# Basis table of a quarter period, layer 0 as a dense product before its mixing, and fp32r parts in place of fp32

## Time and profile before

| what | value |
|---|---|
| median of 3 runs | 227.8 us |
| the profiled execution's own time | 227.68 us |
| its span, first to last instruction | 225.5 us |
| PE busy | 220.1 us (98%) |
| DVE, ACT, POOL busy | 98.8, 75.0, 110.1 us |
| moved by DMA | 20.42 MB, 91 GB/s in the mean |

### The profile page before, as it was taken

One profiled execution on the slowest core, in us unless ns is written; L12 is line 12 of the kernel. 1 busy time (PEld: TensorE's weight loads), 2 busy tenths in 40 slices (PEclk: granted clock), 3 DMA queues, 4 the chain that ended last, 5 costly groups with the idle time before them and its releaser, 6 DMA issues.

```text
span 225.5 us, 3597 instructions
## 1 busy us (share of the span) xinstructions
PE 220.1 (98%) x1212; PEld 185.2 (82%) x1212; DVE 98.8 (44%) x147; ACT 75.0 (33%) x199; POOL 110.1 (49%) x133
## 2 busy tenths in 40 slices
PE   7799999999999999999999999999999999999995
PEld 2568888888888888888888888888888888888884
DVE  4246444344544343445443444454434444544334
ACT  2067233333322333333223333332233333322211
POOL 4757754355566545445665454456654544522200
PEclk9999999999999999999999999999999999999999
DMA  6931022333222323322233323221232332212112
GB/s 201 310 99 52 9 96 96 102 93 84 72 53 96 99 96 99 99 63 88 52 96 99 96 99 99 71 81 52 96 99 96 99 99 81 73 49 90 47 49 93
DMA packets 13543, 20.42 MB, mean 91 GB/s; under 512 B 2618, under 2 KB 4538, under 8 KB 13538
## 3 DMA queue, kind: packets, MB, share of 16 engines
q1 hardware_dynamic: 10642, 18.16, 25.3%
q0 software_dynamic: 2048, 1.05, 2.4%
q10 hardware_dynamic: 848, 1.14, 1.5%
HBM read 11.96 MB, written 8.39 MB: 90 GB/s over the span
## 4 chain that ended last, share of the span: by engine, by line
PE 95%; DMA 3%; DVE 0%; ACTq 0%; issue 0%
PE f_ps L443 26%; PE y_ps L423 26%; PE f_ps L453 13%; PE f_ps L460 13%; PE f_ps L465 13%; DMA basis_sb<-in_fourier_basis 3%; PE a_ps L481 2%; PE a_ps L408 1%; PE y_ps L417 0%; DVE x L392 0%; PE a_ps L460 0%; PE f_ps L417 0%; PE a_ps L465 0%; ACTq L260 0%; ACTq L259 0%
## 5 line engine op out<-in xcount | busy, mean ns | idle before, releaser
L224 POOL TENSOR_TENSOR x<-x_in,bias 128x512 f32<-128x512 f32 x32 | 40.9, 1278 | 81.0 <-issue 46.9
L217 POOL DMA_INDIRECT gathered<-in_L_cond_weights,row_now x58 | 56.5, 974 | 13.2 <-issue 10.1
L443 PE MATMUL f_ps<-a_high,y_high 128*128 128x512 f32 x128 | 53.8, 420 | 0.0
L443 PE MATMUL f_ps<-a_low,y_high 128*128 128x512 f32 x128 | 50.3, 393 | 0.0
L358 DVE TENSOR_TENSOR x<-f_ps,x 128x512 f32<-128x512 f32 x32 | 22.1, 692 | 49.4 <-PE f_ps L443 47.9
L286 ACT ACTIVATE y_high<-y_ps 128x512 fp32r<-128x512 f32 x32 | 19.1, 597 | 69.6 <-PE y_ps L423 69.6
L282 ACT ACTIVATE y_high<-y_ps 128x512 fp32r<-128x512 f32 x32 | 19.1, 597 | 61.4 <-PE y_ps L423 61.4
L460 PE MATMUL f_ps<-b_sign,y_high 128*128 128x512 f32 x124 | 36.5, 415 | 0.0
L423 PEld LDWEIGHTS y_ps<-blocks,x_in 128*128 128x128 f32 x256 | 33.5, 191 | 3.5 <-issue 0.7
L423 PEld LDWEIGHTS y_ps<-blocks,x 128*128 128x128 f32 x256 | 33.4, 191 | 3.2 <-DVE x L358 0.5
L453 PE MATMUL f_ps<-a_high,y_low 128*128 128x512 f32 x128 | 35.1, 396 | 0.0
(11 more groups left out here) (44 smaller groups left out, 73.0 us busy)
## 6 DMA issues: line engine op xcount, KB each, us to landing
x_in<-in_x SPq DMA_DIRECT2D x31, 256.0 KB, 2.7
out_x<-x SPq DMA_DIRECT2D x31, 256.0 KB, 2.0
gathered<-in_L_cond_weights,row_now POOLq DMA_INDIRECT x58, 2.4
w_sb<-in_L_ffn_W_base SPq DMA_DIRECT2D x1, 512.0 KB, 7.5
w_sb<-in_L_ffn_W_base ACTq DMA_DIRECT2D x1, 512.0 KB, 8.9
basis_sb<-in_fourier_basis SPq DMA_DIRECT2D x1, 257.0 KB, 3.3
basis_sb<-in_fourier_basis ACTq DMA_DIRECT2D x1, 257.0 KB, 6.7
bias<-in_L_ffn_b_base SPq DMA_DIRECT2D x1, 256.0 KB
```

The source lines that it names most:

```text
L217: nc.gpsimd.indirect_dma_start(gathered[:, slot, layer, :], None, mix_rows[layer], IndirectOffsetOnAxis(rows[:, layer:layer + 1].bitcast(u ...
L224: nc.gpsimd.tensor_tensor(out=x1[:, slot, :], in0=x_in[:, slot, :], in1=bias[:, :], op=ALU.add).then_inc(biased, 1)
L443: last = nc.tensor.matmul(f0_ps[:, :], y0_high[:, k * P:(k + 1) * P], a[:, k, :], start=(k == 0 and a is a_high), stop=(k == CHUNKS - 1 an ...
```

## The change

- The basis table has a quarter period (129 columns) for all 512 coefficients, half the bytes of before, in one DMA. The product with it is eight matmuls into four banks; DVE builds the four quarters of the spectrum from sums and differences.
- `enc` is loaded twice, to rows 0 and 64 of one tile, and turned into one fp32r tile: high part above, low part below. The spectrum, too, is split. enc x spectrum is then two fp32r products for each of the four banks.
- `masks` goes first in ACT's queue, `kinds` second, then the two `enc` loads, half of `W_base` and the first transposed tile. On DVE `row_of`, which the gathers wait for, comes after `decode`. 13 warm-up matmuls stand in place of 18.
- Layer 0 takes `x_t`, each tile of x with its columns on the partitions (an additional input, laid out by the host), splits it and multiplies it by `A` first (12 matmuls, into `z_ps`). The product is split (`z_high`, `z_low`) and mixed by three fp32r matmuls of 128x512 with a block matrix that is split as well. `x` itself is loaded for the bias sum only.
- Four buffers (`RING = 4`) in place of three, and pairs for the split tiles. PE's order is new.

```diff
-    return np.ascontiguousarray(f.reshape(P, CHUNKS // 2, 2, HALF).transpose(2, 0, 1, 3).astype(np.float32))
+    return np.ascontiguousarray(f.reshape(P, CHUNKS, QUARTER).astype(np.float32))
...
-            sp.dma_start(basis_sb[:, 1], basis[1]).then_inc(basis_loaded[1], 16)
+            sp.dma_start(basis_sb[:, :, :], basis).then_inc(basis_loaded, 16)
             load_w(sp, 0)
-            sp.wait_ge(enc_zero, 1)
-            sp.dma_start(enc_sb[0:R, :], enc).then_inc(enc_loaded, 16)
+            sp.dma_start(xt_in[:, 1, :], xt_tiles[1]).then_inc(xt_loaded[1], 16)
             sp.dma_start(bias[:, :], b_base.partition_broadcast(P)).then_inc(bias_loaded, 16)
-            sp.dma_start(x_in[:, 1, :], x_tiles[1]).then_inc(x_loaded[1], 16)
+            sp.dma_start(x_in[:, 0, :], x_tiles[0]).then_inc(x_loaded[0], 16)
+            sp.dma_start(xt_in[:, 2, :], xt_tiles[2]).then_inc(xt_loaded[2], 16)
...
             def load(tile, slot):
-                sp.wait_ge(mixed0, tile - RING + 1)
+                sp.wait_ge(xt_low_ready, tile - RING + 1)
+                sp.dma_start(xt_in[:, slot, :], xt_tiles[bass.ds(tile, 1)].rearrange("a p t -> (a p) t")
+                             ).then_inc(xt_loaded[slot], 16)
                 sp.wait_ge(biased, tile - RING + 1)
...
+            act.dma_start(masks_sb[:, :, :, :], masks).then_inc(masks_loaded, 16)
             act.dma_start(kinds[:, :, :], kinds_in).then_inc(kinds_loaded, 16)
-            act.dma_start(masks_sb[:, :, :], masks).then_inc(masks_loaded, 16)
-            act.dma_start(basis_sb[:, 0], basis[0]).then_inc(basis_loaded[0], 16)
+            act.wait_ge(enc_zero, 1)
+            for first in (0, ENC_LOW):
+                act.dma_start(enc_sb[first:first + R, :], enc).then_inc(enc_loaded, 16)
             load_w(act, 1)
-            act.dma_start(x_in[:, 0, :], x_tiles[0]).then_inc(x_loaded[0], 16)
+            act.dma_start(xt_in[:, 0, :], xt_tiles[0]).then_inc(xt_loaded[0], 16)
...
+            spectrum_side(0)
+            spectrum_side(1)
+            high_xt(0, 0, 0, recycled=False)
             for k in range(CHUNKS):
                 act.wait_ge(a_done, k + 1)
                 nc.scalar.activation(a_high[:, k, :], a_ps[k][:, :], ACT.Copy).then_inc(a_high_ready, 1)
+            high_xt(1, 1, 0, recycled=False)
+            split_mix(0, 0)
...
         @block.scalar
...
+            def step(tile, u, turn, early=False, new=True):
+                high_y(tile, u, recycled=not early or u >= PAIR)
+                split_mix((u + 2) % RING, turn + (u + 2) // RING)
+                if new:
+                    high_xt(tile + 3, (u + 3) % RING, turn + (u + 3) // RING)
+                high_z(tile + 2, (u + 2) % RING)
+                expand1((u + 2) % RING, tile + 2, recycled=not early or u >= 2)
+                expand0((u + 2) % RING, tile + 2)
...
+            def low_xt(tile, slot, recycled=True):
+                dve.wait_ge(xt_high_ready, tile + 1)
+                if recycled:
+                    dve.wait_ge(fed0, tile - 1)
+                nc.vector.tensor_tensor(out=xt_low[:, slot % PAIR, :], in0=xt_in[:, slot, :],
+                                        in1=xt_high[:, slot % PAIR, :].bitcast(f32), op=ALU.subtract).then_inc(xt_low_ready, 1)
...
         @block.vector
...
+            def step(tile, u, early=False, new=True):
+                low_y(tile, u, recycled=not early or u >= PAIR)
+                low_mix(tile + 2, (u + 2) % RING)
+                if new:
+                    low_xt(tile + 3, (u + 3) % RING)
+                low_z(tile + 2, (u + 2) % RING)
+                residual1(tile, u)
+                residual0(tile + 1, (u + 1) % RING)
...
-            warm_up(18)
+            warm_up(13)
...
+            def feed0_begin(tile, slot, early=False, first=False):
+                pe.wait_ge(xt_high_ready, tile + 1)
+                if not early:
+                    pe.wait_ge(z_low_ready, tile - 1)
+                for k in (0, 1):
+                    if first:
+                        pe.wait_ge(a_low_ready, k + 1)
+                    for a in (a_high, a_low):
+                        nc.tensor.matmul(z_ps[slot % PAIR][:, :], xt_high[:, slot % PAIR, k * P:(k + 1) * P], a[:, k, :],
+                                         start=(k == 0 and a is a_high), stop=False)
+                pe.wait_ge(xt_low_ready, tile + 1)
+                for k in (0, 1):
+                    nc.tensor.matmul(z_ps[slot % PAIR][:, :], xt_low[:, slot % PAIR, k * P:(k + 1) * P], a_high[:, k, :],
+                                     start=False, stop=False)
...
+            def mix0(tile, slot, first=False):
+                pe.wait_ge(expanded, 2 * PER_TILE * (tile + 1))
+                pe.wait_ge(z_high_ready, tile + 1)
+                if not first:
+                    pe.wait_ge(x1_ready, tile)
+                for part in range(2):
+                    nc.tensor.matmul(f0_ps[:, :], blocks0[:, slot, part, :], z_high[:, slot % PAIR, :],
+                                     start=(part == 0), stop=False)
+                pe.wait_ge(z_low_ready, tile + 1)
+                nc.tensor.matmul(f0_ps[:, :], blocks0[:, slot, 0, :], z_low[:, slot % PAIR, :],
+                                 start=False, stop=True).then_inc(mixed0, 1)
...
         @block.tensor
...
+            def step(tile, u, early=False):
+                feed0_begin(tile + 2, (u + 2) % RING)
+                mix1(tile, u, early=early)
+                feed0_end((u + 2) % RING)
+                if early and u == 0:
                     pe.wait_ge(b_ready, 1)
                 else:
-                    pe.wait_ge(out_ready, tile - 1)
-                feed1_high(tile)
-                feed1_low(tile)
+                    pe.wait_ge(out_ready, tile)
+                feed1(tile, u)
+                mix0(tile + 1, (u + 1) % RING)
...
+            mix0(TILES - 1, 3)
+            mix1(TILES - 2, 2)
+            mix1(TILES - 1, 3)
             pe.wait_ge(out_ready, TILES - 2)
-            feed1_high(TILES - 1)
-            mix1_tile(TILES - 1, (TILES - 1) % RING)
-            feed1_low(TILES - 1)
+            feed1(TILES - 2, 2)
             for half in range(2):
-                feed1_high(TILES, end_ps[half], halves[half])
-            for half in range(2):
-                feed1_low(TILES, end_ps[half], halves[half])
+                feed1(TILES - 1, 3, end_ps[half], halves[half])
```

More of the change, by code:

```diff
@@ new lines, in expand0, with high_xt @@
+            def expand0(slot, tile):
+                act.wait_ge(mix_low_ready, tile + 1)
+                for j in range(PER_TILE):
+                    part = slice(j * C, (j + 1) * C)
+                    nc.scalar.activation(blocks0[part, slot, :, part], mix0_parts[part, slot, :, :].bitcast(f32),
+                                         ACT.Copy).then_inc(expanded, 1)
+            def high_xt(tile, slot, turn, recycled=True):
+                act.wait_ge(xt_loaded[slot], 16 * turn + 16)
+                if recycled:
+                    act.wait_ge(fed0, tile - 1)
+                nc.scalar.activation(xt_high[:, slot % PAIR, :], xt_in[:, slot, :], ACT.Copy).then_inc(xt_high_ready, 1)
@@ L309, in _ @@
+            for u in range(RING):
+                step(u, u, 0, early=True)
+            with act.Fori(1, TURNS - 1) as turn:
+                for u in range(RING):
+                    step(turn * RING + u, u, turn)
+            step(TILES - 4, 0, TURNS - 1)
+            step(TILES - 3, 1, TURNS - 1, new=False)
+            high_y(TILES - 2, 2)
+            high_y(TILES - 1, 3)
         @block.vector
@@ L442, in high @@
                     for a in (a_high, a_low):
-                        last = nc.tensor.matmul(f0_ps[:, :], y0_high[:, k * P:(k + 1) * P], a[:, k, :],
-                                                start=(k == 0 and a is a_high), stop=(k == CHUNKS - 1 and a is a_low))
-                    return last
-                for k in range(CHUNKS - 1):
-                    high(k)
-                pe.wait_ge(y0_low_ready, count)
-                if first:
-                    pe.wait_ge(a_high_ready, CHUNKS)
@@ new lines, in mix1, with feed1 @@
+            def mix1(tile, slot, early=False):
+                pe.wait_ge(x1_ready, tile + 1)
+                if not early:
+                    pe.wait_ge(y_low_ready, tile - 1)
+                for k in range(CHUNKS):
+                    last = nc.tensor.matmul(y_ps[slot % PAIR][:, k * P:(k + 1) * P], x1[:, slot, k * P:(k + 1) * P],
+                                            blocks1[:, slot, :], start=True, stop=True)
+                last.then_inc(mixed1, 1)
+            def feed1(tile, slot, to=f1_ps[:, :], columns=slice(0, T)):
+                pe.wait_ge(y_high_ready, tile + 1)
@@ L486, in _ @@
-            feed0(1, first=True)
-            mix0_tile(1, 1, 0)
-            def step(tile, u, turn, first=False):
-                mix1_tile(tile - 1, u % RING)
-                feed0(tile + 1)
```

(10 more changed lines are left out.)

405 lines of the change are left out of this document (225 added, 180 removed).

## The result

The changed kernel takes 226.92 us (median of 20 executions, 223.07 to 228.22); the kernel before took 227.89 beside it (20 executions, 227.10 to 229.27). The ratio is 0.987, 95% interval 0.985 to 0.990. The forecast was 222.1, range 220.4 to 225.2. The direction holds; the size does not: 4.8 us of the expected 5.7 are missing from the median.

What follows compares the result with a forecast made beforehand. PE was taken as the bound, busy 98% of the span. H 13.4 + 14.47 to the first step's end + 29 x 6.26 (181.5) + 10.47 = 219.9 span, plus 2.18 outside it: 222.1 us, range 220.4 to 225.2.

Steps and rivals of the forecast that it cites:

- The tile: Steady loop step: three fp32r matmuls replace mix0 in fp32, 6.45 to 6.26 us a tile, with no added wait.
- The start up to H: Start: basis product at 6.0, W_base landed at about 10.3, then the x_t tile's DMA sets H at 13.4.
- H: Start of ACT's first a_high copy: forecast 13.4 us, bounds 12.0 to 15.3.
- one of the signs that I had named for being wrong: At the start: H set by a_done instead of by the DMA of x_t.
- the clock falls at the start: Rival, start: transposes alone from 7.9 to 11.3, with two pauses, lower PE's clock; 2.2 us lost, 224.3; chance 0.12.
- The matmul spacing of 0.42 behind 8 us: Sign of being wrong: PE's matmuls at the lower clock level's spacing after 8 us.
- two pauses: Start: PE's two pauses around the transposes between 7.9 and 11.3 us, part of the clock rival.
- The rival's price: Clock rival's cost at the start: upper level back after 4.96 us, 2.2 us lost, 224.3 in all.
- enc x spectrum, 0.47 per bank: Start, on PE: enc x spectrum in fp32r takes 0.47 us for each of four banks.
- the first step's end: End of mix0(1), which closes the loop's first step: forecast 14.47 us behind H.
- "Slower: DVE and POOL get in each other's way": Rival, every tile: low_xt waits for add_bias, mix1 stalls 0.2 to 0.6 us, 234 in all; chance 0.07 including other waits.
- The end: From the last of the 29 steps to the span's end: 10.47 us, against 11.56 for today's stretch from mix1(30).

Runs made afterwards that it cites:

- e5: Changed kernel with both e1's filling and e3's wait: 223.31 us (one execution of 433.55), ratio 0.978 to the kernel before.
- e2: Changed kernel with ten transposes filling PE's pause between the two halves of W_base's transposes: 224.35 us, ratio 0.985 to the kernel before.
- e6: e5 with the second enc x spectrum product on all 128 rows in place of 64: 223.17 us, ratio 0.980 to the kernel before.
- e4: e5 with add_bias of each looped tile held to start a little behind low_xt's start: 223.71 us, ratio 0.983 to the kernel before.
- e9: e5 with add_bias of each looped tile held to start a little ahead of low_xt: 222.89 us, ratio 0.978 to the kernel before.
- e1: Changed kernel with 18 bf16 matmuls on zeros filling PE's pause between W_base's transpose halves: 225.80 us, ratio 0.988 to the kernel before.
- e7: e6 with x_t's tile 0 loaded earlier and SP's later loads held until W_base's first half landed: 221.98 us, ratio 0.975.
- e3: Changed kernel with the last four tiles' add_bias waiting for their blocks, pause unfilled: 223.60 us, ratio 0.982 to the kernel before.
- e8: e3 with PE held before the second half of W_base's transposes until xt_high(0) is made: 228.91 us, ratio 1.005 to the kernel before.
- e10: e1 with a short POOL memset between the gather and add_bias of tile 28: 224.87 us, ratio 0.987 to the kernel before.

## Why the prediction was wrong, step by step

- **The tile: right.** 6.45 to 6.25 (forecast 6.26), mix0 in 0.69 (0.70), no wait of PE in a steady step, everything else hidden. In e5's profile 29 such steps take 180.96.
- **The start up to H: the number right by luck, the path wrong.** The basis product began at 5.89 (6.0) and `xt_high(0)` at 12.47 was ended by the DMA of `x_t`, as forecast. But H, 13.48 (13.4), was set by PE's first bank, one of the signs that I had named for being wrong. In the profiles of e2 to e5 H stands 0.53 or 0.54 behind the start of `xt_high(0)`; here that would be 13.0, so that some 0.5 of H is the clock's as well (an estimate). W landed at about 11.05, as late as before, not at 10.3: the fewer bytes ahead of it brought nothing, and PE's pause grew by it.
- **The rival "the clock falls at the start" was the main case, and I gave it 0.12.** This is the first step that failed, and the larger: a term put at nothing in the sum. The matmul spacing of 0.42 behind 8 us, which I had named as a sign of it, came (0.43, 18.73 to 19.16). I set before's pause of 1.42, which kept the clock, beside "two pauses" whose lengths I did not work out; my own times (products done at 7.9, transposes of one half by 8.9, the other half of W at 10.3) gave 1.4, and the DMA's 0.75 of lateness made most of the rest to 2.29. The rival's price failed too: I let the upper level come back after 4.96 us, the records show 10 us at 0.50, and 3.95 lost behind H, with the 0.5 ahead of it 4.4, in place of 2.2. The Trainium skill (TensorE: Matmul & The Clock Gate, Part 4: PE-mode transpose), which I cited for this rival, says that transposes do not count for the clock as other matmuls do; e2 speaks against it: ten more of them in the pause held the clock in all four executions, where 8 of 26 held it without. Of the two things that I had named, transposes alone and pauses, the runs point to the pause.
- **enc x spectrum, 0.47 per bank: mis-sized,** 0.855 at full clock. At full clock H to the first step's end takes 15.09 and not 14.47; e6 showed the cause of the spacing, but the 0.62 is not closed by it in the total, since `low_xt(0)` and `a_low` come late in its profile. What makes it up stays open.
- **"Slower: DVE and POOL get in each other's way": the mechanism is there, the place and the price were not.** It was placed in every tile at 0.2 to 0.6; in steady tiles `add_bias` is over long before, and e4 and e9 show that a forced meeting there costs PE nothing: in e9 residual0 is still 0.26 early. It cost 1.9 in one tile, where the last tiles no longer wait for row names, a branch that the forecast did not walk through and whose wait it put at nothing; this is the second step that failed. At the start it goes with some 1.2 more in four of the profiles at full clock; in the changed kernel's own `low_xt(0)` took 1.50 there, but was done before PE wanted it. The Trainium skill (SBUF — State Buffer, SBUF: two separate sides) has the exclusive lock, which goes to whichever operation starts first; e4 and e9 agree with it (1.64 and 1.18 us). At tile 28 `low_xt`'s record starts 0.53 ahead and it lost, which the rule as I read it does not cover.
- **The end: right,** 10.47.

Sum: 4.4 (clock), 0.6 (enc and what else is late at the start) and 1.9 (tile 28), less 0.4 (H without the clock, 13.0 for 13.4) and 0.4 (the other 28 steps), make 6.1, by which the span passed the forecast's 219.9. The profiled execution's time, 227.82, lies 5.7 above 222.1, because it is 1.8 more than its span where I had added 2.2. The median lies 4.8 above because in half of the executions the clock falls for a shorter time or not at all. That this depends on when W lands in each is argued from the lengths of the pauses in the profiles, not shown execution by execution.

## What to carry to other kernels

When an edit makes a phase ahead of a DMA shorter, write down how long TensorE then stands still, and price the clock for what comes behind, not only the wait; if the wait can't go, fill it with matmuls or transposes, and see that the filling does not itself stand ahead of work that is ready (e1's and e7's profiles). When two engines may exclude each other, walk through the start and the loop's last iterations too, where waits that keep them apart are missing. A forecast number that comes out, such as H, is confirmed only when the row that ends the wait is the one that was named.

## What the hardware showed that I had not expected

- Pauses of TensorE at the start and the clock behind them, one profile each: 1.33 (e3), 1.42 (before) and 1.49 us (e1, with the filling behind it), 1.00; 2.29 (after) and 4.42 (e8), down to 0.50 although PE was busy again, for 10 us after the former. With the pause filled the mean clock was 0.996 or more in all 40 executions (e1, e2, e4 to e7, e9, e10); without, it was lower in 15 of 20 (after) and 3 of 6 (e3).
- fp32r matmuls of 512 columns whose weights change between 128 and 64 rows stand 0.43 apart at full clock (e2, e5), with 128 rows throughout 0.23 (e6).
- A DVE operation with two SBUF inputs beside a gather on POOL keeps its 0.69 us in the steady tiles, but one that begins beside a gather and is not done when the next `add_bias` begins waited for the whole of `add_bias` (3.64 in after, 3.70 in e10; at the start 2.19 to 2.40 in e1, e6, e9 and e10). In e3 and e5 `low_xt(0)` was done by then and kept 0.68.
